# A gated cross-attention block: the first norm's roots in three groups, padding on GpSimd, two halves normalised by ScalarE

## The reference

```python
x = x + tanh(g_xattn[0]) * xattn0(layernorm(x), ctx, ctx)   # 16 heads of 16, softmax, projections Wq, Wk, Wv, Wo
x = x + tanh(g_ffn[0])   * ffn0(layernorm(x))               # 8 experts (silu(x Wg) * (x Wu)) Wd, weighted by routing
x = x + tanh(g_xattn[1]) * xattn1(layernorm(x), ctx, mask)  # one head of 256
x = x + tanh(g_ffn[1])   * ffn1(layernorm(x))               # top-1 gate, capacity of 256 tokens for each expert
layernorm(x) = (x - mean(x)) / sqrt(var(x) + 1e-5)          # over the 256 features
```

## Time and profile before

| | us |
|---|---|
| median of three runs | 704.65 |
| profiled execution, its own time | 703.35 |
| its span | 701.6 |
| TensorE busy | 629.4 (90%) |
| VectorE busy | 470.3 (67%) |
| ScalarE busy | 385.7 (55%) |
| GpSimd busy | 305.6 (44%) |

### The profile page before, as it was taken

How to read it: one execution, slowest core, us unless ns; L and a number is a source line. 1 busy time by engine, 2 the same in 40 slices (tenths; PEclk the granted TensorE clock), 3 DMA queues, 4 the chain that set the end, 5 groups by cost and what they waited for, 6 DMA issues and landing times.

```text
span 701.6 us, 12831 instructions
## 1 busy us (share of the span) xinstructions
PE 629.4 (90%) x4574; PEld 534.2 (76%) x4574; DVE 470.3 (67%) x1220; ACT 385.7 (55%) x610; POOL 305.6 (44%) x336
## 2 busy tenths in 40 slices
PE   4768688899798999999999889899988989999995
PEld 4546467788687788887788777889877764999995
DVE  6996988777966956656956654648557784555552
ACT  4333356577566767776757525444465432665751
POOL 3463846669683353743246224011041422454642
PEclk9988979999989999999999999999999999999998
DMA  7501232443634233423434343334222173945600
GB/s 195 183 16 66 74 135 84 166 171 137 240 150 146 95 121 133 139 91 122 165 121 161 140 151 135 121 126 161 91 93 104 44 266 117 311 172 182 222 16 29
DMA packets 43480, 94.54 MB, mean 135 GB/s; under 512 B 3535, under 2 KB 24399, under 8 KB 42400
## 3 DMA queue, kind: packets, MB, share of 16 engines
q1 hardware_dynamic: 41360, 87.64, 36.5%
q0 software_dynamic: 2064, 6.16, 2.5%
HBM read 72.96 MB, written 21.04 MB: 134 GB/s over the span
## 4 chain that ended last, share of the span: by engine, by line
PE 62%; DVE 25%; issue 7%; ACT 4%; DMA 1%; ACTq 0%; POOL 0%; SPq 0%; DVEq 0%; POOLq 0%
PE psum L1679 40%; PE psum L2236 7%; PE psum L1795 2%; PE psum L2163 2%; PE psum L1765 2%; DVE x_all L1174 2%; DVE work L1154 2%; PE psum L1759 2%; DVE work L1138 1%; DVE work L1035 1%; PE psum L1742 1%; DVE work L1139 1%; DVE arena L1163 1%; PE psum L1802 1%; PE psum L1719 1%
## 5 line engine op out<-in xcount | busy, mean ns | idle before, releaser
L1679 PE MATMUL psum<-arena 128*128 128x256 f32 (+1 forms) x2544 | 438.6, 330 | 24.3 <-DVE x_all L1174 7.0
L1679 PEld LDWEIGHTS psum<-arena 128*128 128x128 f32 x2544 | 375.7, 194 | 69.8 <-issue 8.2
L2277 POOL TENSOR_TENSOR diag<-neg_ident,work 128x1024 fp32r<-128x1024 f32 x32 | 60.9, 1904 | 106.7 <-DVE work L1101 99.6
L1154 DVE TENSOR_TENSOR work<-work,psum 128x512 f32<-128x512 f32 x64 | 43.8, 685 | 68.8 <-PE psum L1679 48.6
L2320 POOL TENSOR_TENSOR arena<-work,arena 128x512 fp32r<-128x512 f32 x34 | 43.8, 1289 | 91.5 <-ACT arena L669 91.5
L669 ACT ACTIVATE arena<-work 128x512 fp32r<-128x512 f32 x64 | 40.3, 630 | 64.4 <-DVE work L1154 57.0
L1174 DVE SCALAR_TENSOR_TENSOR x_all<-psum,w_exp,x_all 128x256 f32<-128x256 f32 x128 | 55.8, 477 | 28.5 <-PE psum L1679 27.9
L662 ACT ACTIVATE work<-psum 128x512 f32<-128x512 f32 x64 | 38.1, 595 | 36.5 <-PE psum L1679 35.9
L2236 PE MATMUL psum<-arena 128*128 128x256 f32 x384 | 47.9, 284 | 0.0
L623 ACT ACTIVATE work<-psum 128x1024 f32<-128x1024 f32 x32 | 32.9, 1027 | 26.5 <-PE psum L1765 22.2
L2236 PEld LDWEIGHTS psum<-arena 128*128 128x128 f32 x384 | 46.5, 191 | 0.0
(11 more groups left out here) (211 smaller groups left out, 884.6 us busy)
## 6 DMA issues: line engine op xcount, KB each, us to landing
arena<-kept SPq DMA_DIRECT2D x24, 1024.0 KB, 5.6
work<-in_w SPq DMA_DIRECT2D x16, 1024.0 KB, 7.6
kept<-arena SPq DMA_DIRECT2D x8, 1536.0 KB, 6.0
arena<-kept SPq DMA_DIRECT2D x24, 512.0 KB, 4.9
work<-in_w SPq DMA_DIRECT2D x8, 768.0 KB, 8.2
slots<-fill POOLq DMA_DIRECT2D x1, 2080.0 KB
work<-in_ctxT SPq DMA_DIRECT2D x8, 256.0 KB, 3.0
work<-in_ctxT SPq DMA_DIRECT2D x4, 512.0 KB, 5.6
```

The costliest lines, as they stand in the source:

```text
L1154: dve.tensor_tensor(gu[i % 2], gu[i % 2], ps[:, UP, :], ALU.mult).then_inc(hm, 1)
L1679: mm = pe.matmul(dst, left(i, k), right(j, k), start=(n == 0), stop=(n == 3 * K2 - 1))
L2277: pool.tensor_tensor(diag, neg_ident[:, :].rearrange("p (o q) -> p o q", o=1).to_broadcast([P, 8, P]), mx[u % 2].rearrange("p (h o) -> p h ...
```

## The change

Means, variances and roots of the first norm now have buffers for all 16 tiles (`mv0`, `rstd0`). VectorE makes the roots in three groups: tiles 0 and 1, then 2 to 5, both before step 0, and 6 to 15 at the end of step 2; the moments of tiles 6 to 15 are made in step 2. For the latter two groups it also makes `shift0`, the mean times minus the root. ScalarE normalises halves 2 and 3 from these, in steps 1 and 3, behind a wait on `rooted`; the others stay on VectorE. The root on GpSimd goes. In the head `masks_ready` stands ahead of the norm of half 1; GpSimd fills the padding as its first work, and makes `k_masks(1)` behind the diagonal of piece 1. The second bias scaling moves to the end of step 2, with the filling of `fill`. SyncE loads the mask ahead of tiles 2 to 5, now one transfer, and 6 to 15 last.

```diff
-        rscratch = sb("rscratch", 2)
+        mv0 = sb("mv0", 2 * B).rearrange("p (n s) -> p n s", s=2)
+        rstd0 = sb("rstd0", B)
...
+        shift0 = rt[2][:, 0:B]
...
-        def reciprocal_root(dve, step, var, r, t):
+        def reciprocal_root(dve, step, var, r, t, u):
             step(dve.tensor_scalar(t, var, EPS, None, ALU.add))
             step(dve.tensor_scalar(r.bitcast(I32), t.bitcast(I32), -0.5, float(0x5f3759df), ALU.mult, ALU.add))
             for _ in range(3):
-                step(dve.tensor_tensor(u := scratch[:, 0:r.shape[1]], r, r, ALU.mult))
+                step(dve.tensor_tensor(u, r, r, ALU.mult))
...
-        ROOTS = [b for b in range(2 * GB, STEPS) if norm_at(b)]
...
-            x_load(1, 2, 4)
             sp.dma_start(mask0_raw, mask0.rearrange("a p n -> p a n")).then_inc(s_mask0, 16)
+            x_load(1, 2, 6)
             weights(3)
...
-            x_load(2, 4, B)
+            x_load(2, 6, B)
...
+            def normalise0(h):
+                act.wait_ge(rooted, h - 1)
+                act.wait_ge(xt_tr, h)
+                for i in range(2):
+                    t = 2 * h + i
+                    act.activation(xn0[i], x_all[:, t, 0:D], ACT.Identity, bias=shift0[:, t:t + 1], scale=rstd0[:, t:t + 1]
+                                   ).then_inc(ln0, 1)
...
                 if b % 2:
+                    normalise0(nxt)
                     ctx_high(nxt)
...
-            def values_ready():
-                for p in range(2):
-                    su.done(dve.memset(v0[p][:, :, :, DH + 1:32], 0.0))
-                    su.done(dve.memset(v0[p][:, :, :, DH:DH + 1], 1.0))
-
             def bias_ready():
                 dve.wait_ge(s_tanh, 1)
                 dve.tensor_scalar(bo0r, bo0r, tgate[:, 0:1], None, ALU.mult).then_inc(s_bo, 1)
+
+            def fill_ready():
                 dve.tensor_scalar(bv1r, bv1r, tgate[:, 1:2], None, ALU.mult).then_inc(s_bo, 1)
-
-            def fill_ready():
                 su.done(dve.memset(fill[:, 0:ROW - 1], 0.0))
                 dve.memset(fill[:, ROW - 1:ROW], float(2 * T)).then_inc(s_bo, 1)
...
             def moments0(h):
-                dve.wait_ge(s_x[min(h, 2)], 16)
+                dve.wait_ge(s_x[(0, 1, 1, 2, 2, 2, 2, 2)[h]], 16)
                 for i in range(2):
                     vs.done(dve.bn_stats(stats[:, i, :], x_all[:, 2 * h + i, 0:D]))
                 dve.wait_ge(vs.sem, vs.last)
                 for i in range(2):
-                    vs.done(dve.bn_aggr(mv[:, i, :], stats[:, i, :]))
+                    vs.done(dve.bn_aggr(mv0[:, 2 * h + i, :], stats[:, i, :]))
                 dve.wait_ge(vs.sem, vs.last)
...
-            def root0():
-                reciprocal_root(dve, step, mv[:, 0:2, 1:2].rearrange("p n o -> p (n o)"), rstd[:, 0:2], newton[:, 0:2])
+            def root0(first, tiles):
+                sel = slice(first, first + tiles)
+                reciprocal_root(dve, step, mv0[:, sel, 1:2].rearrange("p n o -> p (n o)"), rstd0[:, sel], rt[0][:, 0:tiles],
+                                rt[1][:, 0:tiles])
+                if first:
+                    dve.scalar_tensor_tensor(shift0[:, sel], mv0[:, sel, 0:1].rearrange("p n o -> p (n o)"), -1.0, rstd0[:, sel],
+                                             ALU.mult, ALU.mult).then_inc(rooted, 1)
 
             def normalise0(h):
                 if h:
                     dve.wait_ge(xt_tr, h)
                 for i in range(2):
-                    normalise(2 * h + i, i, xn0[i], ln0)
-
-            def norm0(h):
-                moments0(h)
-                root0()
-                normalise0(h)
+                    t = 2 * h + i
+                    normalise(t, mv0[:, t, 0:1], rstd0[:, t:t + 1], xn0[i], ln0)
...
+                if h < 2:
+                    dve.wait_ge(padded, 2 * h + 2)
...
             weights_low(0)
-            norm0(0)
+            moments0(0)
+            root0(0, 2)
+            normalise0(0)
             constants_ready()
             weights_low(1)
             weights_low(2)
             dve.wait_ge(s_bias, 16)
             k_low(0, GA)
             xn_low(0, TL)
-            norm0(1)
             masks_ready()
+            moments0(1)
+            moments0(2)
+            root0(2, 4)
+            normalise0(1)
             maximum(0)
             dve.wait_ge(su.sem, su.last)
             q_low(0, DN)
             k_low(1, GA)
             xn_low(1, TL)
             weights_low(3)
-            values_ready()
             dve.wait_ge(s_small, 16 * 7)
             v_add(0, UP)
 
...
                 if b > 1:
                     x1_low(b - 2)
                 maximum(2 * b + 1)
+                if b == 2:
+                    moments0(3)
+                    moments0(4)
                 if b:
                     o_normalise(b - 1)
-                if b % 2:
-                    moments0(nxt)
-                else:
+                if b == 2:
+                    moments0(5)
+                    moments0(6)
+                if b % 2 == 0:
                     q_low(nxt, GA)
                 if b:
                     o_low(b - 1)
-                if b % 2:
-                    root0()
                 maximum(2 * b + 2)
-                if b % 2:
-                    normalise0(nxt)
                 if b:
                     residual(b - 1)
                 else:
                     bias_ready()
-                if b == 1:
-                    fill_ready()
                 if b % 2:
                     k_low(nxt, GA)
                     xn_low(nxt, UP)
                 else:
                     v_add(nxt, UP)
+                if b == 2:
+                    moments0(7)
+                    root0(6, 10)
+                    fill_ready()
...
-                if norm_at(b):
-                    if b in ROOTS:
-                        moments0_for_gpsimd(norm_at(b))
-                    else:
-                        moments0(norm_at(b))
...
-                if norm_at(b) and b not in ROOTS:
-                    root0()
...
-                    if b in ROOTS:
-                        dve.wait_ge(rooted, ROOTS.index(b) + 1)
...
-            def root0(b):
-
-                n = ROOTS.index(b)
-                pool.wait_ge(mom, 2 * n + 2)
-                pool.wait_ge(ln0, 2 * norm_at(b))
-                root_of_both()
-                pool.sem_inc(rooted, 1)
...
+            for p in range(2):
+                pool.memset(v0[p][:, :, :, DH + 1:32], 0.0).then_inc(padded, 1)
+                pool.memset(v0[p][:, :, :, DH:DH + 1], 1.0).then_inc(padded, 1)
             ctx0_low(0)
             pool.wait_ge(s_const, 16)
             pool.wait_ge(s_setup.sem, 3)
             k_masks(0)
             ctx0_low(1)
             diagonals(0)
-            k_masks(1)
 
             for b in range(STEPS):
                 fa, fb = experts_of(b)
                 nxt = (b + 1) // 2 + 1
                 if b < B:
                     diagonals(2 * b + 1)
+                if b == 0:
+                    k_masks(1)
...
-                if b in ROOTS:
-                    root0(b)
```

More of the change, by code:

```diff
@@ L299, in block_kernel @@
         xb_ok = sem("x_with_bias")
-        mom, rooted = sem("moments_ready"), sem("root_ready")
-        rt_step = Steps(sem("gpsimd_root_step"), 0)
+        padded, rooted = sem("values_padded"), sem("roots_ready")
         vs = Steps(sem("vector_step"), 0)
@@ L1043, in moments0 @@
                 for i in range(2):
-                    vs.done(dve.bn_aggr(mv[:, i, :], stats[:, i, :]))
+                    vs.done(dve.bn_aggr(mv0[:, 2 * h + i, :], stats[:, i, :]))
                 dve.wait_ge(vs.sem, vs.last)
-            def moments0_for_gpsimd(h):
-                for i in range(2):
-                    vs.done(dve.bn_stats(stats[:, i, :], x_all[:, 2 * h + i, 0:D]))
-                dve.wait_ge(vs.sem, vs.last)
-                for i in range(2):
-                    dve.bn_aggr(mv[:, i, :], stats[:, i, :]).then_inc(mom, 1)
-            def root0():
-                reciprocal_root(dve, step, mv[:, 0:2, 1:2].rearrange("p n o -> p (n o)"), rstd[:, 0:2], newton[:, 0:2])
+            def root0(first, tiles):
[5 more added lines that the diff above has]
+                                             ALU.mult, ALU.mult).then_inc(rooted, 1)
             def normalise0(h):
@@ L1141, in norm1 @@
                     dve.wait_ge(x1t, b)
-                normalise(b, 2, xn1, ln1)
+                normalise(b, mv[:, 2, 0:1], rstd[:, 2:3], xn1, ln1)
             def x1_low(b):
@@ L1264, in root_a @@
                 reciprocal_root(dve, step, mvA[:, sel, 1:2].rearrange("p n o -> p (n o)"), rstdA[:, sel],
[L1265 removed]
+                                newtonA[:, 0:groups * GB], scratch[:, 0:groups * GB])
                 dve.scalar_tensor_tensor(shiftA[:, sel], mvA[:, sel, 0:1].rearrange("p n o -> p (n o)"), -1.0, rstdA[:, sel],
@@ L1455, in root_b @@
                 r = x_all[:, sel, D:D + 1].rearrange("p n o -> p (n o)")
```

(2 more changed lines are left out.)

18 lines of the change are left out of this document (2 added, 16 removed).

## The result

The changed kernel takes 699.87 us, median of six runs (698.72 to 701.51), against 704.49 for the kernel before beside it: 4.6 us less, a ratio of 0.9941 (95% interval 0.9914 to 0.9967). That is faster, but the forecast was 691.2 and its range ended at 697: two thirds of the gain are missing.

A forecast was written before the change was run, and what follows sets the result against it. The prediction took the head's VectorE chain, step 7's root and low clock after waits as the bounds. Head -7.5 and step 7 -6.0 sum to -13.5 from 704.65: 691.2 us, range 685.5 to 697.

The forecast's parts named there:

- Step 7: Step 7 without VectorE's root: waits for h_mult and the key rest go, and the low clock; -6.0 us.
- q_low(0): Head: with one diagonal beside it, q_low(0) takes 2.2 us for 3.78; -1.5 us.
- step 1's own gain: Step 1: moments, root and normalisations leave VectorE; 4.6 us more than the 2.4 carried in.
- the piece between the two transposes of step 2: Step 2, transposes of xn1(0) to xn1(1): 16.1 us becomes 15.1.
- maximum(7): End of step 2: this maximum, behind the ten-wide root, comes near 64 us; a sign of being right.
- the root's price: End of step 2: the ten-wide root and work beside it delay maximum(7) and o_normalise(2) by 2.9 us.
- TensorE wait for a normalisation of half 2 or 3: Steps 1 and 3: no such TensorE wait is left; a sign of being right.
- Head: Steps 0 to 3, up to the first expert product: -7.5 us, bounds -11 and -4.
- The first maximum: Head: VectorE no longer waits for scores before the first maximum; -0.4 us.
- the low clock behind the wait: Step 3, behind TensorE's idle 3.6 us before o_back(2): products cost 0 to 3.3 us more, 2.0 taken.
- Step 8: Step 8: GpSimd's roots and VectorE's moments go; priced at 0.
- step 7 is not the root's: Rival: h_mult is free, but another wait replaces it and the clock still falls; only 2.25 go: 695; chance 0.13.

The follow-up runs named there:

- before_late_pin: Kernel before, with GpSimd's low part of the third context group waiting for VectorE's low part of the last expert; 704.46 us against 704.19.
- ones_later: Changed kernel with the moments of half 1 put between the masks and ones_r in VectorE's program; 699.90 us against 700.04.
- head_b1: Changed kernel with tiles 2 to 7 in the second root group and 8 to 15 made in step 4; 693.84 us, 6.0 less.
- masks_later: Changed kernel with GpSimd's masked keys of half 5 moved from step 7 to step 8; 696.24 us, 3.6 less.
- no_root7: Kernel before with the moments and root of half 5 left out of step 7; 700.29 us against 704.36.
- root_again: Changed kernel with the moments and two-tile root of half 5 made once more in step 7; 705.84 us against 700.04 on the other chip.
- mid_pin: Changed kernel with GpSimd's subtractions of expert 4's weights in step 6 waiting for VectorE's low part of expert 3; 694.07 us, 5.8 less.
- late_pin: Changed kernel with GpSimd's low part of the third context group waiting for VectorE's low part of the last expert; 695.95 us, 3.9 less.
- three: Changed kernel with the edits of late_pin, mid_pin and masks_later together; 693.27 us.

## Why the prediction was wrong

**Right.** Step 7 was -6.0 and is -6.7, for the reason given: neither wait is left. But 2.7 us of this hang on the execution, in step 7's low clock, which `before_late_pin` doesn't have there; against it the step gives 4.0, and that the sum came so near is in part luck. `q_low(0)` takes 2.2 us; step 1's own gain was 4.6, measured 4.4; the piece between the two transposes of step 2 was to be 15.1 us and is 14.9 (45.26 to 60.12); `maximum(7)`, behind the ten-tile root, is at 64.86 (64 forecast), and the root's price was +2.9, measured +2.5; ScalarE's normalisations, the fills on GpSimd and the new order of loads cost 0. No TensorE wait for a normalisation of half 2 or 3 is left.

**Head: -7.5, measured -5.4 at the first expert product** (90.01 for 95.40). Two terms were mis-sized. The first maximum was put at -0.4 and is at +0.9. `ones_r`, 1.32 us where it took 0.22 before and 0.26 in `ones_later`, accounts for most, and `hide`, 0.75 us where it took 0.29, for the rest. I read how the masks collide in GpSimd's rows for `q_low` and not for `masks_ready`, which I moved past the same engine. This 1.3 us is carried on: the sum took 2.4 us into step 1, and 1.05 are measured there. And the low clock behind the wait was taken at 2.0 us of 0 to 3.3; it cost 3.0: from the wait's end to the values' products (L1790, 75.12) it is 8.4 us, and 5.4 for the same products in `head_b1` at the full clock. The prediction set the Trainium skill's rule beside this (TensorE: Matmul & The Clock Gate, HAM oscillation): by it the whole 3.3 us fall due. The trace agrees, 7.5 us at a granted clock of 0.54 behind the wait of 3.31 us.

**Step 8: "0", measured +3.1.** This step of the working was wrong, not only mis-sized. I took step 11 as the pattern for step 7 without its root and asked only whether TensorE had room. I didn't ask when GpSimd's split for the next step would be ready once TensorE came 6.7 us sooner; the earlier trace rows already had GpSimd busy 22.65 us in step 7, and step 7 was to shrink to 24.6. `masks_later` and `no_root7` show it for 1.58 us of wait. The other 1.5 us are low clock in step 8, and for them the cause stays open: twelve of the fourteen profiles have it, `before_late_pin` and `root_again` with the root in step 7 among them, and only those of the kernel before and of `masks_later` don't.

**Step 6 and 514 us: not in the sum at all, 2.75 and about 5 us.** The prediction treated what lies behind step 8 as carried along unchanged. But two subtractions on VectorE stand so close to a start of GpSimd's that a shift of 0.2 us changes which one waits. `mid_pin` and `late_pin` give 2.6 us in the step and 3.9 us of the time. Of the rivals none named it; "step 7 is not the root's" is nearest in time (695) and has another mechanism. At 514 us the hold makes 2.2 us of the loss, and 2.6 are a low clock that followed the same hold in the changed kernel and not in `head_b1`.

The Trainium skill states the rule for this (SBUF — State Buffer, Who interferes with whom): VectorE and GpSimd share a pair of ports, a VectorE instruction with two inputs in SBUF contends with a GpSimd one that reads SBUF, and the issue order decides who blocks. The trace agrees on order at 514 us: 0.08 us ahead, 0.69 us; 0.10 us behind, 2.79 us. In step 6 it doesn't settle it, since VectorE began 0.29 us ahead of the subtractions, but behind GpSimd's casts, and was held. Used in the prediction, the rule would have asked how near to each L1163 a start of GpSimd's lay; at 521 us that was 0.08.

**By the sum of what was measured:** 5.7 (head, to step 4) - 1.0 (step 4, where the clock is low from 81.5 to 95.5, before from 88.5 to 99.0) + 1.9 (step 5, where only the kernel before has the low clock, 129.5 to 133.5) - 2.75 (step 6) + 6.7 (step 7) - 3.1 (step 8) = 7.4; less 5.4 from 514 to 537 us, and 1.4 back: 3.4, and 3.5 us of span, 4.6 by the medians.

What stays open: where TensorE's clock falls behind waits that all kernels share. Of these stretches the prediction counted two in the kernel before; its trace has six (47.5 to 58, 78.5 to 82, 88.5 to 99, 129.5 to 133.5, 191 to 198, 549.5 to 553). One near 404 to 427 us, worth some 2.5 us, came in six of the twelve experiments' profiles and in neither profile of the changed kernel; the one in step 8 came with the wait for the split and without it (`three`). The kernel before and `before_late_pin`, the same program up to 521 us, differ in both. No run here tells what decides it.

## What to carry to other kernels

When a step gets shorter, ask of every other engine what it has to deliver at the start of the next step, and whether its own work still fits: otherwise part of the gain becomes a wait in the next step. Look for pairs of instructions on VectorE and GpSimd that both read two buffers and start within a few tenths of a microsecond of each other: any shift of the program can turn their order, so pin it with one wait, GpSimd behind VectorE's short instruction, before timing anything else. A root of ten tiles cost what one of two does (eleven instructions in 2.2 us at 61.64, in 2.1 us at 7.12), so the question is only where it stands: beside a long run of products (step 4, 27.7 us for 27.3) it was nearly free, in front of a maximum it cost 2.5 us and a stretch at the low clock. And profile a kernel more than once before a step's time is split into causes: the same program gave 31.3 and 28.6 us for step 7.

## What was not expected of the hardware

- A VectorE instruction can be held for more than one GpSimd instruction: 4.35 us in step 6, through four subtractions of 0.7 us each and an addition of 0.73, until GpSimd's chain ended at 146.40.
- Beside GpSimd's casts it is hardly held: at 148.45 before the change it took 0.70 us within four casts, which took 1.90 us for 1.43; in `mid_pin`, 0.96 us behind the first cast, it took 1.03.
- A root's small instruction takes 0.17 us at 128 x 10 elements and 0.16 at 128 x 2: here the width costs next to nothing.
- Waits of the same length were followed by a low clock in one profile and not in another: 1.56 us near 201 in `three` and in `masks_later`. So it is even in one program: a wait of 2.32 us ends at 420.73 in the kernel before and at 420.40 in `before_late_pin`, which differ only from 521 us on, and the 42 products behind it take 8.50 us in the first and 11.08 in the second, with the clock low from 420 to 427.
